# FFN block 1 computed with seven products instead of eight, its weight parts made during the attention's last unit

## The reference

```python
# x: (2, 512, 512); 32 query heads, 8 key/value heads of 128, window of 128, causal
xn = layernorm(x)
q, k, v = xn @ wq, xn @ wk, xn @ wv          # rope on q and k
s = softmax(mask(q k^T / sqrt(128))) v @ wo
deq = lambda w, z, sc: (w - z) * sc          # z, sc per group of 128 rows of w
gate = silu(xn @ deq(gate_w, gate_z, gate_s))   # 512 x 1792
up   = xn @ deq(up_w, up_z, up_s)               # 512 x 1792
g = silu((gate * up) @ deq(down_w, down_z, down_s))
out = x + s * g
```

## Time and profile before

| | |
|---|---|
| median of 3 timed runs | 876.59 us (876.36 to 878.03) |
| the profiled execution | 877.88 us, its span 875.5 us |
| granted clock, mean over the span | 0.994 of 2.4 GHz |
| PE busy | 863.8 us (99%) |
| DVE, POOL, ACT busy | 673.5, 578.6, 493.1 us |
| matmuls | 4340 |
| chain that ended last | PE 93%, DVE 4% |

### The profile page before, as it was taken

One profiled execution on the slowest core, in us unless ns is written; L12 is line 12 of the kernel. 1 busy time (PEld: TensorE's weight loads), 2 busy tenths in 40 slices (PEclk: granted clock), 3 DMA queues, 4 the chain that ended last, 5 costly groups with the idle time before them and its releaser, 6 DMA issues.

```text
span 875.5 us, 14447 instructions
## 1 busy us (share of the span) xinstructions
PE 863.8 (99%) x4340; PEld 728.3 (83%) x4340; DVE 673.5 (77%) x1263; ACT 493.1 (56%) x1322; POOL 578.6 (66%) x501
## 2 busy tenths in 40 slices
PE   8899999999999999999999999999999999999997
PEld 7788888888888888888888888888888888888886
DVE  8686777778776878778777867777765898989876
ACT  4566565665566566556556565665574444444533
POOL 4565567666676666666576757764446887887865
PEclk9899999999999999999999999999999999999999
DMA  8021011130003012100301030114374464655542
GB/s 267 9 61 49 25 37 30 32 97 24 24 24 108 24 36 72 48 24 24 96 24 26 22 108 24 36 48 132 110 204 120 134 182 142 173 152 164 162 133 96
DMA packets 94851, 72.25 MB, mean 83 GB/s; under 512 B 4192, under 2 KB 80480, under 8 KB 94816
## 3 DMA queue, kind: packets, MB, share of 16 engines
q1 hardware_dynamic: 94096, 70.70, 27.6%
q10 hardware_dynamic: 720, 1.11, 0.3%
HBM read 63.41 MB, written 8.39 MB: 82 GB/s over the span
## 4 chain that ended last, share of the span: by engine, by line
PE 93%; DVE 4%; ACT 1%; issue 1%; POOL 1%; DMA 0%; DVEq 0%
PE ps L38 30%; PE ps L39 29%; PE ps L40 29%; PE ps L1099 3%; PE ps L1079 1%; ACT probs L1242 1%; DVE ps L1505 0%; DMA y<-L_attn_x 0%; DVE kept L1538 0%; DVE work L1501 0%; DVE work L1500 0%; DVE stats L1433 0%; POOL pt_lo L1372 0%; DVE xt_lo L1469 0%; DVE work L1507 0%
## 5 line engine op out<-in xcount | busy, mean ns | idle before, releaser
L38 PE MATMUL ps<-xt_hi,w_lo 128*128 128x512 f32 x412 | 164.9, 400 | 0.4 <-POOL w_lo L209 0.4
L39 PE MATMUL ps<-xt_lo,w_hi 128*128 128x512 f32 x412 | 161.9, 393 | 0.0
L40 PE MATMUL ps<-xt_hi,w_hi 128*128 128x512 f32 x412 | 161.0, 391 | 0.0
L1372 POOL TENSOR_TENSOR pt_lo<-kept,pt_hi 128x512 fp32r<-128x512 f32 x112 | 142.9, 1295 | 26.8 <-ACT pt_hi L1253 26.4
L1367 POOL TENSOR_TENSOR q_lo<-work,q_hi 128x512 fp32r<-128x512 f32 x64 | 82.7, 1293 | 93.0 <-ACT q_hi L1225 93.0
L1242 ACT ACTIVATE probs<-ps,neg_max 128x128 f32<-128x128 f32 x256 | 90.5, 366 | 42.5 <-DVE neg_max L1525 42.5
L1253 ACT ACTIVATE pt_hi<-kept 128x512 fp32r<-128x512 f32 x112 | 69.2, 632 | 66.2 <-DVE kept L1538 66.2
L38 PE MATMUL ps<-wo_hi,o_lo 128*128 (+1 forms) x256 | 99.7, 390 | 0.1
L39 PE MATMUL ps<-wo_lo,o_hi 128*128 (+1 forms) x256 | 99.6, 389 | 0.0
L40 PE MATMUL ps<-wo_hi,o_hi 128*128 (+1 forms) x256 | 99.6, 389 | 0.0
L40 PEld LDWEIGHTS ps<-xt_hi,w_hi 128*128 128x128 f32 x412 | 77.8, 189 | 17.1
(11 more groups left out here) (173 smaller groups left out, 2236.8 us busy)
## 6 DMA issues: line engine op xcount, KB each, us to landing
work<-L_attn_wq SPq DMA_DIRECT2D x32, 256.0 KB, 2.8
work<-L_attn_wo SPq DMA_DIRECT2D x32, 256.0 KB, 2.7
work<-L_ffn_gate_w SPq DMA_DIRECT2D x14, 256.0 KB, 3.7
work<-L_ffn_gate_z SPq DMA_DIRECT2D x14, 256.0 KB, 4.6
work<-L_ffn_gate_s SPq DMA_DIRECT2D x14, 256.0 KB, 5.6
work<-L_ffn_up_w SPq DMA_DIRECT2D x14, 256.0 KB, 3.3
work<-L_ffn_up_z SPq DMA_DIRECT2D x14, 256.0 KB, 3.9
work<-L_ffn_up_s SPq DMA_DIRECT2D x14, 256.0 KB, 4.6
```

The lines of the kernel that those rows point to most:

```text
L38: pe.matmul(out, stat[1], mov[0], start=first, stop=False, skip_group_check=grown)
L39: pe.matmul(out, stat[0], mov[1], start=False, stop=False, skip_group_check=grown)
L40: return pe.matmul(out, stat[0], mov[0], start=False, stop=last, skip_group_check=grown)
L1372: pool.tensor_tensor(pt_lo[:, w, :], kept[:, w, :], pt_hi[:, w, :].bitcast(F32), ALU.subtract).then_inc(pt_split, 1)
```

## The change

Block 1 becomes one of the blocks of seven products. It is number 0 of 13 now (`FIRST_BLOCK = 1`, `BLOCKS = 13`). Its UP and GATE are dequantised in (1, 1) and (1, 2) of the last unit; ACT makes their high parts in (1, 2), POOL the low part of UP in (1, 2) and the combinations in (1, 3), ACT the high parts of these in (1, 3). Since `gate_row` lies over tiles of the attention, this block's GATE uses DOWN's row, and DOWN of block 0 is dequantised after the last addition to `y`. There is no pair before it, so no DOWN products stand between its products, and P6 comes before P5. SP loads the same pieces in the same order, UP before GATE in block 1; DOWN of block 1 is no longer loaded by a line of its own ahead of the loop. In the first unit ACT's order changes (first roped query before the table load for Exp, the two halves of the tiles around the fourth piece), and the fifth piece's low part moves from POOL to DVE, behind the first of the four tiles there. The functions `row`, `hi_up` and others only get the block's number as an argument.

```diff
@@ -116,12 +116,10 @@
 FIRST = [(GATE, 0), (UP, 0)]
-IN_BODY = [(GATE, 1, 0), (UP, 1, 0), (DOWN, 0, 0), (UP, 0, 1), (GATE, 0, 1), (DOWN, 1, 0)]
-
-
-EARLY = 3
+IN_BODY = [(UP, 1, 0), (GATE, 1, 0), (DOWN, 0, 0), (UP, 0, 1), (GATE, 0, 1), (DOWN, 1, 0)]
+
+
 EARLY_LOADS = 5
-EARLY_PRODUCTS = 2
 EARLY_MIDDLES = 2
@@ -188,7 +186,7 @@
         sh, s = self.sh, k % Shared.RING
...
-SEVEN_FROM = 1
-BLOCKS = 2 * (PAIRS - SEVEN_FROM)
+FIRST_BLOCK = 1
+BLOCKS = NI - FIRST_BLOCK
+
+
+def pair_of(blk):
+
+    return divmod(blk + FIRST_BLOCK, 2)
+
+
 U1, U2, G2, S1, S2, S3, S4 = range(7)
...
-    def row(self, kind):
-        return self.gate_row[:, :] if kind == GATE else self.sh.work[:, self.ROW_UP if kind == UP else self.ROW_DOWN, :]
+    def row(self, kind, blk):
+
+        if kind == GATE and blk:
+            return self.gate_row[:, :]
+        return self.sh.work[:, self.ROW_UP if kind == UP else self.ROW_DOWN, :]
...
-            dve.wait_ge(sh.w_split, self.index_of(blk - 1, DOWN) + 1)
+            dve.wait_ge(sh.w_split, (self.index_of(blk - 1, DOWN) if blk >= 0 else self.index_of(0, GATE)) + 1)
         elif blk > 0:
             dve.wait_ge(self.s_split, 2 * blk - 1)
         else:
-            dve.wait_ge(sh.w_split, FfnWeights.index(SEVEN_FROM - 1, 1) + 1)
-        row = self.row(kind)
+
+            dve.wait_ge(sh.w_split, FfnWeights.index(0, -1) + 1)
+        row = self.row(kind, blk)
...
@@ -473,24 +482,35 @@
         if blk >= 2:
             pe.wait_ge(self.seven_silu, 2 * blk - 2)
         elif blk == 0:
-            pe.wait_ge(sh.silu_done, (SEVEN_FROM - 1) * 4 + 3)
+            pe.wait_ge(sh.silu_done, 1)
         else:
-            pe.wait_ge(sh.mid_done, (SEVEN_FROM - 1) * 4 + 4)
+            pe.wait_ge(sh.mid_done, 2)
         self.product(pe, blk, U1, a, True, self.b_of(0, 0))
         if blk:
             pe.wait_ge(self.seven_mid, 2 * blk - 1)
         else:
-            pe.wait_ge(sh.mid_done, (SEVEN_FROM - 1) * 4 + 3)
+            pe.wait_ge(sh.mid_done, 1)
         self.product(pe, blk, U2, self.B, True, self.b_of(1, 0))
+        def fifth():
+            if blk:
+                pe.wait_ge(self.seven_mid, 2 * blk)
+            else:
+                pe.wait_ge(sh.silu_done, 2)
+            self.product(pe, blk, S1, self.C, True, self.t_of(T1))
+
+        def sixth():
+            pe.wait_ge(self.copied, 3 * blk + 1)
+            self.product(pe, blk, S2, a, False, self.t_of(T2))
+
+        pe.wait_ge(self.s_split, 2 * blk + 2)
         if blk:
-            pe.wait_ge(self.seven_mid, 2 * blk)
+            fifth()
+            sixth()
         else:
-            pe.wait_ge(sh.silu_done, (SEVEN_FROM - 1) * 4 + 4)
+
             pe.wait_ge(sh.sums_in, 3 * 4 * 16)
-        pe.wait_ge(self.s_split, 2 * blk + 2)
-        self.product(pe, blk, S1, self.C, True, self.t_of(T1))
-        pe.wait_ge(self.copied, 3 * blk + 1)
-        self.product(pe, blk, S2, a, False, self.t_of(T2))
+            sixth()
+            fifth()
...
@@ -506,7 +526,7 @@
     def copy(self, act, blk, i):
-        act.wait_ge(self.made, 7 * blk + (self.DONE_P1, self.DONE_P6, self.DONE_P7)[i])
+        act.wait_ge(self.made, 7 * blk + (self.DONE_P1, self.DONE_P6 if blk else self.DONE_P5, self.DONE_P7)[i])
         wait(act, self.added, 3 * blk - (2, 0, 1)[i])
         act.activation(self.copies[:, i, :], self.bank(self.A[blk % 2]), ACT.Copy).then_inc(self.copied, 1)
...
         def moves(sp):
-            fw.load_next(sp, sv.index_of(-1, DOWN), DOWN, -1)
             for blk in range(BLOCKS):
-                if blk + 1 < BLOCKS:
+
+                if 1 < blk + 1 < BLOCKS:
                     fw.load_next(sp, sv.index_of(blk + 1, UP), UP, blk + 1)
                     fw.load_next(sp, sv.index_of(blk + 1, GATE), GATE, blk + 1)
                 fw.load_next(sp, sv.index_of(blk, DOWN), DOWN, blk)
...
-            for e in range(EARLY_PRODUCTS, 4):
-                gate_up(0, e)
             for blk in range(BLOCKS):
+                n, ii = pair_of(blk)
                 def downs(which):
                     for t in which:
-                        down(SEVEN_FROM + blk // 2, 4 * (blk % 2) + t)
+
+                        if n:
+                            down(n, 4 * ii + t)
                 sv.products(pe, blk, downs)
             for t in range(TT - 1):
                 down(PAIRS, t, True)
...
-            sv.hi_up(act, 0)
             act.wait_ge(sh.y_ready, NKV * TT)
-            hi_of_mid(0, *ORDER[0])
-            hi_of_mid(0, *ORDER[1])
-            sh.silu(act, 0, 2)
-            sv.hi_gate(act, 0)
-            sv.hi_s(act, 0, 0)
-            sv.hi_s(act, 0, 1)
-            hi_of_mid(0, *ORDER[2])
+            hi_of_mid(0, 0, 0)
+            hi_of_mid(0, 0, 1)
             sv.hi_down(act, -1)
-            sh.silu(act, 0, 3)
-            hi_of_mid(0, *ORDER[3])
             for blk in range(BLOCKS + 1):
...
-            sv.lo_up(pool, 0)
-            split_mid(0, *ORDER[0])
-            split_mid(0, *ORDER[1])
-            sv.lo_gate(pool, 0)
-            split_mid(0, *ORDER[2])
+            split_mid(0, 0, 0)
+            split_mid(0, 0, 1)
             sv.lo_down(pool, -1)
-            split_mid(0, *ORDER[3])
             for blk in range(BLOCKS + 1):
...
             dve.wait_ge(sh.pt_split, NKV * BATCH * (2 * QB - 1))
             for e in range(EARLY_MIDDLES):
@@ -749,14 +747,9 @@
             dve.wait_ge(sh.y_ready, NKV * TT)
             dve.tensor_tensor(sh.y[:, TT - 1, :], ps[:, 7, :], sh.y[:, TT - 1, :], ALU.add)
-            sv.dequantise(dve, 0, GATE)
-            for e in range(EARLY_MIDDLES, 4):
-                dve.wait_ge(mid_split, e - 1)
-                sh.middle(dve, 0, e)
-                if e == EARLY_MIDDLES:
-                    sv.dequantise(dve, -1, DOWN)
+            sv.dequantise(dve, -1, DOWN)
             for blk in range(BLOCKS + 1):
-                more, n, ii = blk + 1 < BLOCKS, SEVEN_FROM + blk // 2, blk % 2
+                more, (n, ii) = blk + 1 < BLOCKS, pair_of(blk)
...
-        FFN_AT = {(0, 3): (-1,), (1, 0): (0,), (1, 1): (1,), (1, 2): (2,)}
+        FFN_AT = {(0, 3): (-1,)}
...
@@ -1291,15 +1284,16 @@
             hi_of_roped(0, 0, 0)
             scale(1)
+            hi_of_roped(0, 0, 1)
             act.wait_ge(root_done, 2)
             act.activation(preload[:, 0:1], first[1][:, 0:1], ACT.Exp)
-            hi_of_roped(0, 0, 1)
             hi_of_roped(0, 0, 2)
-            hi_of_x(1)
+            hi_of_x(1, range(0, 2))
             hi_of_roped(0, 0, 3)
+            hi_of_x(1, range(2, GROUP))
+            hi_of_roped(0, 0, 4)
             act.wait_ge(proj_ready, V_ + 1)
             act.activation(v_t[:, :], bank(0, V_), ACT.Copy).then_inc(v_drained, 1)
-            hi_of_roped(0, 0, 4)
             hi_of_v(0, 0)
...
                         hi_of_o(n)
+                        if last and (b, j) == (1, 2):
+
+                            act.wait_ge(scores_ready, UNITS * QB)
+                            sh.seven.hi_up(act, 0)
+                            sh.seven.hi_gate(act, 0)
+                        if last and (b, j) == (1, 3):
+                            for i in range(2):
+                                sh.seven.hi_s(act, 0, i)
...
-            for i in range(5):
+
+            for i in range(4):
                 lo_of_roped(0, 0, i)
...
+                        if last and (b, j) == (1, 2):
+                            sh.seven.lo_up(pool, 0)
+                        if last and (b, j) == (1, 3):
+                            sh.seven.lo_gate(pool, 0)
...
-            lo_of_x(1)
+            lo_of_x(1, range(0, 1))
+            dve.wait_ge(rope_hi, 5)
+            hi, lo = rope_target(0, 4)
+            dve.tensor_tensor(lo, by_group(row_of(0, 0, 4), 4), hi.bitcast(F32), ALU.subtract).then_inc(rope_split, 1)
+            lo_of_x(1, range(1, GROUP))
...
+                        if last and (b, j) in ((1, 1), (1, 2)):
+                            sh.seven.dequantise(dve, 0, UP if j == 1 else GATE)
```

More of the change, by code:

```diff
@@ L327, in __init__ @@
         self.t_hi = sb("t_hi", [P, 4, 2, 512], F32R)
-        pair_of = lambda which: [sb(f"seven_{which}_{part}", [P, 7, 2, P], F32R) for part in ("hi", "lo")]
+        parts_of = lambda which: [sb(f"seven_{which}_{part}", [P, 7, 2, P], F32R) for part in ("hi", "lo")]
+        even = parts_of("even")
         with ExitStack() as over:
             self.res = over.enter_context(nc.sbuf_tensor("res", [P, TT, HID], F32))
-        even = pair_of("even")
         self.s = sb("s_parts", [P, 4, 2 * P])
-        odd = pair_of("odd")
+        odd = parts_of("odd")
         self.w_hi, self.w_lo = (even[0], odd[0]), (even[1], odd[1])
@@ L398, in hi_up @@
             act.wait_ge(self.made, 7 * (blk - 1))
-        act.activation(self.part(self.w_hi, blk, U1, U2), self.row(UP), ACT.Copy).then_inc(self.sh.w_hi_done, 1)
+        act.activation(self.part(self.w_hi, blk, U1, U2), self.row(UP, blk), ACT.Copy).then_inc(self.sh.w_hi_done, 1)
     def hi_gate(self, act, blk):
```

(18 more changed lines are left out.)

41 lines of the change are left out of this document (16 added, 25 removed).

## The result

| | before | after |
|---|---|---|
| median of 20 timed runs each | 876.61 us (874.27 to 878.59) | 879.78 us (877.36 to 882.54) |
| ratio | | 1.0036, 95% interval 1.0026 to 1.0046 |
| the profiled execution | 877.88 us, span 875.5 | 881.78 us, span 879.6 |
| matmuls | 4340 | 4334 |

The changed kernel does six matmuls less and is 0.36% slower. The forecast was 879.2 us and slower. In the profiled executions the change costs 3.9 us, where the sum had +1.3, and the median of after lies 2.0 us under its own profiled execution.

The account below looks back on a forecast made before the run. The prediction took PE, busy 863.8 of 875.5 us, as the bound. From the profiled 877.88 us, the first unit's -4.5 and the passage's +5.8 gave 879.2 us, range 874.5 to 881.3.

Parts of the forecast that it names:

- the sum had +1.3: Whole kernel: first unit -4.5 us and passage to the FFN +5.8 us, added to the profiled 877.88 us.
- The first wait, +3.2: Passage: PE waits 3.2 us before the third product, for a copy queued on ACT behind DOWN's high part.
- By unshared lengths: Passage without DVE and POOL taking turns: DOWN ready at 671.0, passage about +1.2 us, kernel near 874.6 us.
- P4's +0.85: Passage: P4 follows P7 with no down product between, so it waits 0.85 us for the copy.
- P3's +0.35: Passage: P3 waits 0.35 us for the addition of gate2, which stands behind the next DOWN's dequantisation.
- The next block's second product, +1.6: End of passage: this product waits 1.6 us for a middle ready at 685.1; it could start at 683.55.
- The clock at the passage, +1.2: Passage: half clock for 6.8 us after the 3.2 us idleness, adding 1.2 us beyond the waits it absorbs.
- needs 4.0 us ..., so it lands just in time: Passage: the next DOWN's transfer, issued after 673.0, needs 4.0 us behind an issue of about 1 us.
- +5.8 forecast: Passage as a whole: 5.8 us lost, from fewer matmuls (-1.36), four waits and the fallen clock; the upper bound.
- rival 1: Passage stalls but its clock does not fall: passage +4.6 us, kernel 878.0 us; chance 0.15.
- The first unit, -4.5: First unit: scores start 1.2 us earlier, and the clock stays up, giving back 3.3 us: -4.5 us.
- rival 4: First unit: the clock falls anyway at the shorter idleness, only 1.2 us gained; up to 882.5 us; chance 0.17.

Follow-up runs that it names:

- filled passage: The changed kernel with twelve unused matmuls between block 1's second and third product: 879.15 us, ratio to before 1.0032.
- first unit alone: The kernel before with only the first unit's new order of splits, block 1 left plain: 873.34 us, ratio to before 0.9978.
- all copies first: The changed kernel with block 0's DOWN dequantised inside the last unit, and ACT's copies ahead of the next block's high parts: 878.19 us, ratio to before 1.0015.
- gate2 first: The changed kernel with ACT's early first copy, gate2 added before the next DOWN's dequantisation, silus before its high part: 879.27 us, ratio to before 1.0033.
- copy first: The changed kernel with ACT copying block 1's first product before making DOWN's high part: 879.53 us, ratio to before 1.0028.
- early DOWN: The changed kernel with block 0's DOWN dequantised inside the last unit; in block 1 gate2 and silus precede the next DOWN: 878.21 us, ratio to before 1.0021.

## Why the prediction came out as it did

**The first wait, +3.2: right.** It measured 2.99 us (673.80 against 670.81), at the place, after twelve matmuls of `seven_even`, and from the cause that was given: dequantisation in turns with POOL (1.53 and 1.64 us), ACT's high part waiting for it, the copy behind. DOWN was ready at 672.5, forecast 673.0. The Trainium skill (GPSIMD Engine Reference, § 1. Specifications) states a contention of GpSimd with VectorE instructions that have two SBUF inputs. The trace agrees: the next pair of DVE, one at 672.43 with POOL idle and one at 673.14, 0.1 us ahead of POOL's next split, took 0.68 and 0.69 us, and that split 1.74. By unshared lengths the passage would have been +1.2; it measured +4.36.

**P4's +0.85: right,** 0.84 (679.36 to 680.43, less 0.23). **P3's +0.35: too small.** It measured 1.5 us where the clock stays up (678.27 to 680.01 in the kernel with filled passage, less 0.23), and vanished in after, where PE came that much later. **The next block's second product, +1.6: wrong,** it waited in neither. The middle that it needs was ready at 683.73 (683.04 + 0.69) and not at 685.1, and the product started at 684.68. Two things took this wait away: the middle was ready 1.4 us sooner than forecast, and PE came 1.1 us later than 683.55.

**The clock at the passage, +1.2: mis-sized.** It fell, as forecast, but for 3.4 us instead of 6.8. That is the step that failed in the passage's sum: a spell half as long costs PE 1.7 us and not 3.4, and by the forecast's own terms 1.7 us are all taken up by the waits behind P4 (0.35, and most of the 1.6). A second step failed beside it, "needs 4.0 us ..., so it lands just in time". The transfer of DOWN was issued as forecast, right after 672.5, but landed 5.4 us after the issue of its last third began (673.39 to 678.82). So with a full clock P3 would have had to wait for it, as the kernel with filled passage shows, and the spell cost nothing against that. That SP issued the three transfers of the next UP right behind it, and that these slowed it, is a likely reason; it wasn't tried. The whole passage: +5.8 forecast, +4.36 measured; rival 1 had +4.6 from a clock that stays up, and its number is the nearer one, although the clock fell.

**The first unit, -4.5: the mechanism right, its size not.** Done alone it gave 4.65 us in the profiled execution and some 2 to 3 in the middle (ratio 0.9978). In the profile of after it gave 0.25. That execution is rival 4. From the profile of each kernel that has the edits: the start of ACT's first high part that waits for a transfer of the attention's weights, PE's wait before the scores, and the clock of 33 to 40 us:

| kernel | high part starts | PE waits | granted clock 33 to 40 us |
|---|---|---|---|
| first unit alone | 14.23 | 1.45 | 1.00 |
| filled passage | 14.57 | 1.50 | 0.76 |
| all copies first | 14.54 | 1.62 | 0.76 |
| gate2 first | 14.85 | 1.85 | 0.79 |
| copy first | 15.04 | 1.94 | 0.77 |
| after | 15.14 | 2.20 | 0.56 |
| early DOWN | 15.27 | 2.34 | 0.55 |
| first unit alone, with 6 unused matmuls | 14.44 | none | 1.00 |
| early DOWN, with 10 unused matmuls | 15.19 | none | 1.00 |

Where the transfer landed up to 1 us later, the wait is longer by nearly as much, and the clock is full, or half for 3.4 us or for about 7. "1.4 is nearer to the 0.8 that left it up" was a choice between two points. In the first unit 1.45 left the clock up and 1.50 did not, but the length of the wait alone doesn't decide: the old order idled 2.59 us in two profiles, with 6.8 us at half clock in one and 3.4 in the other, and at the passage 1.49 us left the clock up (gate2 first). The forecast treated one execution's start as fixed. The rows are of different kernels, one execution each: that the landing varies as much between the executions of one kernel, and is what spreads their times, is likely but not shown, nor why it varies. A rival is that the changed kernel starts later as such: the eight profiles of it and its variants have 14.5 to 15.3, the four of the kernel before and its variants 14.2 to 14.8.

**Together.** In the middle of many executions the first unit gave 1.9 us by the ratio (forecast 4.5) and the passage cost 5.4 (forecast 5.8): +3.5, where +3.2 was measured for both. So the larger miss of the sum is the first unit's size, 2.6 us. The forecast's +1.3 was added to an execution that lay 1.3 us over the median of before, and 879.2 came within 0.6 us of 879.78. The side and the place of the loss were right; the closeness of the number is in part luck.

**Where the saved 1.36 us went.** The passage has not one wait but a stack of them. By the passage's length in the profiles, taking the first away gave 0.3 us; P3's as well, 1.3; the dequantisation moved out of it, 2.4 in all; after that, the last queue of ACT mended, POOL was the bound. Before, 10.88 us of plain products stood over the other engines' work for the first block of sevens, and POOL was at that work without a pause from 669.24 to 685.9:

```profile
674.01 0.73 POOL L434 TENSOR_TENSOR s_parts<-s_parts,work 128x256 f32<-128x256 f32 x1
674.81 1.10 POOL L436 TENSOR_TENSOR s_parts<-work,s_parts 128x256 f32<-128x256 f32 x1
675.88 1.18 POOL L417 TENSOR_TENSOR seven_even_lo<-gate_row,seven_even_hi 128x256 fp32r<-128x256 f32 x1
677.02 2.54 POOL L417 TENSOR_TENSOR seven_even_lo<-s_parts,seven_even_hi 128x512 fp32r<-128x512 f32 x2
...
684.18 1.74 POOL L417 TENSOR_TENSOR seven_odd_lo<-work,seven_odd_hi 128x512 fp32r<-128x512 f32 x1
```

The change gave the cover away. That POOL's work alone keeps the passage over its old length is shown only for the one order that was tried; another split of work between the engines wasn't.

## What to carry to other kernels

A block with fewer matmuls is worth its saving only where the engines that prepare it have slack; at a change of phase, plain products that need nothing prepared may be the cheapest cover there is. When a profile names one wait there, count what stands behind it in every queue up to the next free stretch, transfers too: here the named 2.8 us were worth 0.3 us. A wait of PE after which its clock falls in some executions is worth filling with unused matmuls (ten took some 1.7 to 2 us off the kernel before), since the loss comes and goes from one execution to the next.

## What the runs showed of the hardware

- PE's clock after a wait, in single profiles. In the first unit: full after 1.45 us, half for 3.4 us or about 7 after 1.50 to 2.34 (seven kernels with the new order); half for 6.8 us in one and 3.4 us in another after 2.59 (old order). At the passage: full after 1.26 to 1.49, half for some 3.4 us after 2.04 (all copies first, 0.71 from 684 to 688 us) and after 2.83.
- The executions of three kernels lie within 4.3 us (before), 3.2 (first unit alone) and 4.4 us (early DOWN); with the wait filled by unused matmuls within 1.2, 1.3 (five executions) and 1.7 us.
- At half clock matmuls of 512 columns went from 0.227 to 0.427 us apart. At the passage that cost nothing, since a transfer was under way over the same stretch.
- The same instruction on DVE, a subtraction or product of 128x512 out of SBUF, took 0.68 us with POOL idle, and mostly 1.1 to 1.7 with POOL at work; POOL's splits went from 1.3 to 1.7.
- The last third of DOWN (three transfers of 256 KB) landed 4.0 us after its issue in the median of before, and 5.4 us at the passage of after, with the next piece issued right behind it. GATE's last third had a median of 5.6 us already in before, in the same stretch, so the 4.0 was no figure for any piece:

```profile
work<-L_ffn_gate_s SPq DMA_DIRECT2D x7, 256.0 KB, 5.6
```
